# Edge attention of a graph network: VectorE weighs the gathered rows with numbers left in PSUM

## The reference, cut to what matters

```python
x_l = (x @ W_l).reshape(n, H, C)
x_r = (x @ W_r).reshape(n, H, C)
m = jax.nn.leaky_relu(x_l[src] + x_r[dst], negative_slope=0.2)
alpha = jnp.einsum('ehc,hc->eh', m, att)
amax = jax.lax.stop_gradient(jax.ops.segment_max(alpha, dst, num_segments=n))
ea = jnp.exp(alpha - amax[dst])
denom = jax.ops.segment_sum(ea, dst, num_segments=n)
w = ea / jnp.maximum(denom[dst], 1e-16)
out = jax.ops.segment_sum(w[:, :, None] * x_l[src], dst, num_segments=n)
```

## Time and profile before

| | us |
|---|---|
| median of 3 runs | 2713.86 |
| lowest and highest of them | 2712.55, 2718.64 |
| the profiled execution, whole | 2709.06 |
| the profiled execution, span from first to last instruction | 2707.4 |

### The profile page before, as it was taken

One profiled execution on the slowest core, in us unless ns is written; L12 is line 12 of the kernel. 1 busy time (PEld: TensorE's weight loads), 2 busy tenths in 40 slices (PEclk: granted clock), 3 DMA queues, 4 the chain that ended last, 5 costly groups with the idle time before them and its releaser, 6 DMA issues. The chain is left out here.

```text
span 2707.4 us, 43473 instructions
## 1 busy us (share of the span) xinstructions
PE 2123.3 (78%) x11554; PEld 1262.0 (47%) x11554; DVE 1774.8 (66%) x5087; ACT 1042.3 (39%) x2345; POOL 1784.7 (66%) x2143
## 2 busy tenths in 40 slices
PE   8999999967778728999987959999999387784000
PEld 3444444435556516666654425666666255452000
DVE  4777767645555549999971115777777576665675
ACT  1111111115555514777774424555555234442000
POOL 3555555567777548888736754777777677665776
PEclk9999999978998959999998989999999699997555
DMA  5755555548999746788748977777664399998999
GB/s 198 234 184 191 182 188 184 185 146 280 313 315 305 263 151 196 246 269 258 249 176 298 410 289 243 234 232 235 218 215 156 103 334 385 370 346 283 376 398 346
DMA packets 331156, 689.12 MB, mean 255 GB/s; under 512 B 48137, under 2 KB 53731, under 8 KB 330913
## 3 DMA queue, kind: packets, MB, share of 16 engines
q1 hardware_dynamic: 219368, 403.36, 43.0%
q0 software_dynamic: 76720, 218.39, 24.5%
q10 hardware_dynamic: 34825, 64.59, 6.5%
HBM read 415.92 MB, written 287.44 MB: 260 GB/s over the span
## 5 line engine op out<-in xcount | busy, mean ns | idle before, releaser
L148 PE MATMUL psum<-wl,xT 128*128 128x512 f32 x632 | 288.8, 600 | 0.0
L148 PE MATMUL psum<-wg,yT 128*128 128x512 f32 x632 | 285.6, 595 | 0.0
L148 PE MATMUL psum<-wr,xT 128*128 128x512 f32 x632 | 284.1, 592 | 0.0
L2125 POOL DMA_INDIRECT xg<-n_rows,ids x219 | 219.3, 1001 | 94.4 <-issue 49.4
L337 ACT ACTIVATE xb<-xa,xsc 128x512 f32<-128x512 f32 x79 | 64.2, 814 | 480.5 <-POOL xsc L397 480.5
L384 POOL TENSOR_TENSOR ve<-mv,epst 128x1 f32<-128x1 f32 x79 | 51.0, 646 | 254.3 <-DVE mv L439 254.3
L1686 POOL DMA_INDIRECT slot_tokens<-sl x158 | 168.8, 1068 | 70.8 <-issue 66.6
L2307 POOL DMA_INDIRECT q<-slot_outputs,qs x158 | 164.6, 1042 | 66.1 <-issue 47.9
L154 PE MATMUL psum<-ident,xg 128*128 128x128 f32 x876 | 140.6, 298 | 68.3 <-DMA xg<-n_rows,ids 33.9
L148 PEld LDWEIGHTS psum<-wr,xT 128*128 128x128 f32 x632 | 120.3, 190 | 150.9 <-issue 150.9
L148 PE MATMUL psum<-wc,x1T 128*128 128x264 f32 x632 | 162.1, 401 | 32.4 <-DVE hb L1231 24.9
(11 more groups left out here) (324 smaller groups left out, 5410.2 us busy)
## 6 DMA issues: line engine op xcount, KB each, us to landing
slot_outputs<-yo ACTq DMA_DIRECT2D x54, 1024.0 KB
x_rows<-x SPq DMA_DIRECT2D x158, 256.0 KB, 3.3
edge_sums<-eo SPq DMA_DIRECT2D x29, 1056.0 KB, 6.6
edge_sums<-go SPq DMA_DIRECT2D x29, 1024.0 KB
xT<-in_xTt SPq DMA_DIRECT2D x79, 256.0 KB
xl_rows<-xl SPq DMA_DIRECT2D x79, 256.0 KB, 3.4
xr_rows<-xr SPq DMA_DIRECT2D x79, 256.0 KB
residual_rows<-xb SPq DMA_DIRECT2D x79, 256.0 KB, 3.8
```

What stands on the lines that cost most here:

```text
L148: last = nc.tensor.matmul(ps, lhs[:, k, :], rhs[:, k, :], start=(k == 0), stop=(k == DK - 1))
L2125: pool.indirect_dma_start(xg[:, t % 8, :], None, XN3, bass.IndirectOffsetOnAxis(ids[:, t:t + 1], 0), bounds_check=NP - 1, oob_is_err=False ...
```

## The change

The tile `wt` and the semaphore `b_wt` are dropped, and with them the first of the three copies in `largest`, together with its wait for `b_v`. `weigh` reads the eight numbers of an edge from bank 2 or 3, columns 128 + 32j to 135 + 32j, where `weights` left them, again repeated over 64 columns. It waits for `b_mo`, which the last copy of `largest` raises, in place of `b_wt`. TensorE's `logits`, which next writes that bank, additionally waits for `b_v`: all four tiles of the quad two before have been weighed.

```diff
-        wt = sb("wt", [P, 2, 4, H], F32, pb)
...
                 def weigh(w):
                     u, j = w // 4, w % 4
-                    dve.wait_ge(b_wt, u + 1)
+                    dve.wait_ge(b_mo, u + 1)
                     if w >= 8:
                         dve.wait_ge(b_s, w - 7)
                     nc.vector.tensor_tensor(heads(vv[:, w % 8, :], CE)[:, :, 0:C], heads(gl[:, w % 16, :]),
-                                            wt[:, u % 2, j, :].unsqueeze(2).to_broadcast([P, H, C]),
+                                            bank[2 + u % 2][:, P + 32 * j:P + 32 * j + H].unsqueeze(2).to_broadcast([P, H, C]),
                                             ALU.mult).then_inc(b_v, 1)
...
                     pe.wait_ge(b_mT, quad(u)[-1] + 1)
                     if u >= 2:
                         pe.wait_ge(b_mo, u - 1)
+                        pe.wait_ge(b_v, 4 * (u - 1))
...
                 def largest(u):
                     h = u % 2
                     act.wait_ge(b_et, u + 1)
-                    if u >= 2:
-                        act.wait_ge(b_v, 4 * (u - 1))
-                    act.activation(wt[:, h, :, :], of_heads(bank[2 + h][:, P:2 * P]), ACT.Copy).then_inc(b_wt, 1)
                     if u >= 2:
                         act.wait_ge(b_s, 4 * (u - 1))
```

More of the change, by code:

```diff
@@ L644, in gnn_ffn @@
         b_md, b_rs, b_st = sems("b_md", 2), sems("b_rs", 2), sems("b_st", 2)
-        (b_m, b_t, b_mT, b_at, b_pf, b_mx, b_d, b_e, b_et, b_wt, b_wo, b_mo, b_S, b_v, b_s, b_r, b_0) = (
-            sem("b_" + n) for n in "m t mT at pf mx d e et wt wo mo S v s r 0".split())
+        (b_m, b_t, b_mT, b_at, b_pf, b_mx, b_d, b_e, b_et, b_wo, b_mo, b_S, b_v, b_s, b_r, b_0) = (
+            sem("b_" + n) for n in "m t mT at pf mx d e et wo mo S v s r 0".split())
         def quad(u):
```

## The result

| | before | after |
|---|---|---|
| median, us | 2713.95 (6 runs) | 2697.43 (6 runs) |
| lowest and highest, us | 2711.05, 2718.64 | 2690.24, 2701.75 |
| profiled execution, whole, us | 2709.06 | 2696.83 |
| its span, us | 2707.4 | 2695.1 |

The ratio is 0.9934, 95% interval 0.9917 to 0.9951: 18 us, between 13 and 23. A second timing on another chip gave 0.9930 (0.9916 to 0.9945). 2704.8 us had been forecast, in a range of 2700 to 2712; the median lies 2.6 us under its lower end.

A forecast was written before the change was run, and what follows sets the result against it. POOL's back-to-back row gathers were taken to bound the edge attention's first stretch. From the 2713.86 us median, 9.3 us less gather stretch and 0.2 us more drain gave 2704.8 us, range 2700 to 2712.

The forecast's parts named there:

- The bound and the mechanism: Edge attention: back-to-back POOL gathers set the first stretch; two-SBUF-operand VectorE instructions stretch them by 29.7 us, a PSUM operand does not.
- The rival by which PSUM frees nothing: Edge attention: gathers wait for any two-input VectorE instruction of this length, so no gain, about 2714 us; chance 0.08.
- If all 236 fare as they do: First stretch: all gathers bear the 0.086 us each of those not asking inside `weigh`; stretch 20.4 us, gain 9.3 us.
- the upper bound of 12.6: First stretch: at most all 12.6 us of gather stretch spent during `weigh` is won.
- The 198 gathers: First stretch: gathers not asking inside `weigh`, taken to bear 17.1 us, all the stretch except the 12.6.
- The row at 834.08: First stretch: a gather of 2.31 us across a `weigh` and the `both` behind it, ending 0.88 us past the latter.
- The later semaphore and the store's landing: `weigh` waiting for `b_mo`: nothing in the first stretch, 0.2 us in the drain; the store's landing stays hidden.
- The rival of the DMA engines and the loop: Edge attention: DMA engines can't carry rows faster (eaten gain, 2709 to 2714 us, chance 0.10), or the ScalarE loop becomes the bound.
- The slow `weigh`: Quad loop: repeated PSUM numbers at half speed, +0.68 us per `weigh`, make the loop the bound, about 2734 us; chance 0.05.

The follow-up runs named there:

- sbuf_late: The changed kernel with ScalarE again copying the weights to `wt` in SBUF and `weigh` reading them there, later semaphore kept; ratio 0.9996 to the kernel before.
- before_look4: The kernel before, unchanged, traced once more; 38.0 us of stretch, first read of the sums at 964.4 us.
- after_again: The changed kernel, unchanged, in a second trace; 14.5 us of stretch, first read of the sums at 945.0 us, drain 34.3 us.
- both_one_input: The changed kernel with `both` copying the left rows alone, right rows still gathered and waited for; ratio 0.9915 to the kernel before.
- weigh_halves: The kernel before, `weigh` still reading `wt` in SBUF, with `weigh` made in two instructions of four heads each; ratio 0.9982.

## Why the prediction was wrong in size

*The bound and the mechanism* were right. POOL set the first stretch, with gaps of 0.30 us in every trace, and its stretch went where it was predicted to go: 40 to 52 gathers a trace asked inside the new `weigh`, none was held. With the operand back in SBUF, and the later semaphore kept, the gain was gone; with ScalarE's copy back and the operand in PSUM, it stayed.

*The rival by which PSUM frees nothing*, and with it the Trainium skill's inference (SBUF — State Buffer, section Who interferes with whom) that a tensor_tensor leaves descriptor generation alone, is answered by sbuf_late and after: 30.1 against 15.6 us of stretch.

*The step that failed* is the one from "If all 236 fare as they do" to "the stretch is 20.4 us, a gain of 9.3 us", and the upper bound of 12.6 beside it. The stretch fell by 14.1 us in the first pair of traces (29.7 to 15.6) and by 33.2 - 15.3 = 17.9 us between the means.

- The base is not where it failed. One execution was read as if it were the program, and it had the least stretch of six; but the same step on the means of the six gives nearly the same gain. There 13.7 us lie at `weigh`, 42 gathers ask inside it, and the other 194 bear 19.5 us, 0.100 each. For 236 gathers that is 23.7 us, a gain of 9.5. The median that the sum started from, 2713.86, was met by the six runs (2713.95).
- What failed is the stretch that remains: 23.7 us by that step, 15.3 measured. The step gave every gather the mean wait of those that had not asked inside `weigh`. As many as before ask inside `both`, 56 a trace in the mean against 55. But what these wait, counted to the end of the wait in whichever instruction it falls, went down from 21.2 to 12.3 us, 0.39 to 0.22 each.
- The step also mixed two counts. It took off the 12.6 us spent during `weigh`, of which 2.4 belong to gathers that had asked in the `both` ahead of it. The 198 gathers bore 19.5 us in that trace and not 17.1; counted so, the step gives a gain of 6.5, further from the result.

One part of the shorter waits is plain. A gather of before_look4 shows it, on POOL's timeline and on VectorE's:

```profile
711.89 2.30 POOL L690 DMA_INDIRECT gr<-xr_rows,idx  x1 [0.30 <-issue]
```

```profile
711.43 0.69 DVE L703 TENSOR_TENSOR me<-gl,gr 128x512 f32<-128x512 f32 x1
712.03 0.68 DVE L741 TENSOR_TENSOR vv<-gl,wt 128x512 f32<-128x512 f32 x1
712.63 0.69 DVE L703 TENSOR_TENSOR me<-gl,gr 128x512 f32<-128x512 f32 x1
```

It asked at 712.01 inside `both`, was passed over at that one's end, again at the end of `weigh`, and ended 0.87 us after the second `both`. In the six traces with `weigh` in SBUF 37 gathers were passed over, and these are the waits over 0.60 us (2.1 to 8.8 us a trace). All 37 had asked about 0.1 us before the end of a `both` that a `weigh` followed without a break, close to the start of that `weigh`. What decides it is not shown: some 50 others that were held in such a `both` were served at its end, a few of them asked at the same distance from it. No gather that had asked elsewhere was passed over; some 200 were held ahead of other seams of two such instructions, and each was served at the first. In the four traces with `weigh` in PSUM a `both` is not followed by a `weigh` that holds gathers, none was passed over, and no wait was longer than 0.53 us. The row at 834.08 was such a chain; the prediction split it between the two lines, and its upper bound counted only the pieces at `weigh`, as if those at the `both` behind had to stay.

Of the 21.2 us, 4.7 were waited after the end of the `both` in which the gather had asked. These are the chains, and they are gone. The other 16.4 us, waited inside that first `both`, became 12.3, 0.30 to 0.22 us each: the gathers meet it nearer to its end. Why they do is not shown.

*The later semaphore and the store's landing* cost the first stretch nothing, as forecast. The drain was put at 0.2 us more and came out at 1.3 (32.0 against 30.7 us in the means), within its own spread of 28.0 to 34.3. Where it was longest among the traces of the change, in after_again, VectorE was late: it adds the last rows 11.9 us after their issue, against 7.5 in after.

*The rival of the DMA engines and the loop* didn't bite at this size, but something of the kind stands close behind: both_one_input lost about half of its further gain in the drain. *The slow `weigh`* fell: 677 ns. The page Perfetto Trace Analysis, section Optimizing Scalar/DVE Operations, of the Trainium skill gives figures by which PSUM would be some 65 ns dearer, an estimate; the trace of after has it 5 ns cheaper (677 against 682).

## What to carry to other kernels

Where POOL issues indirect gathers back to back, lay them beside VectorE's instructions: in these traces one with two operands in SBUF can hold a gather until it ends. Reading one of the operands from PSUM, where it stood anyway, freed the gathers and cost nothing in the instruction's duration (677 ns against 682). Look for such instructions without a break between them, since a gather can lose its turn there, and try shorter ones where they can't leave SBUF. When some meetings of two engines are taken away, the waits at the others change too: don't carry their old mean over into the sum, and don't take the pieces at one instruction for an upper bound. Read several traces for such a sum.

## What the runs showed of the hardware that was not expected

- A waiting gather is not always served at the first seam between two VectorE instructions: 37 gathers in six traces, all of which had asked about 0.1 us before the end of a `both` with a `weigh` right behind, waited over 0.60 us, up to 1.31. What decides it is not shown.
- Two halves of one instruction, back to back, can hold a gather through both (the one of 750.81 in weigh_halves, 1.83 us, which had asked in the `both` ahead of them).
- The same program's stretch varied by 8 us between five executions of the kernel before (29.7 to 38.0). That is 0.3% of its time, and about half of the 17.6 us between the shortest and the longest of the five.
